# Turning the x tile of a token step: TensorE transposes, or VectorE's 32 x 32 blocks with sixteen DMA moves

## What is computed

```
hs = layernorm(x)                                # 4 sequences of 256 tokens
gate, xBC, dt = split(hs @ in_proj_w.T)          # 8192, 8192 + 2*8*128, 128 columns
xBC = silu(causal_conv(xBC, 4 taps) + conv_b)    # x: 128 heads of 64; B, C: 8 groups of 128
dt = softplus(dt + dt_bias);  A = -exp(A_log)
y[l] = sum over s <= l of (C[l] . B[s]) * exp(cumsum(dt A)[l] - cumsum(dt A)[s]) * dt[s] * x[s]  +  D * x[l]
out = rmsnorm(y * silu(gate)) * norm_w @ out_proj_w.T
```

## Time and profile before

| | |
|---|---|
| median of three runs | 1679.8 us (1677.4 to 1680.8) |
| the profiled execution | 1681.4 us, its span 1679.7 us |
| PE busy | 1643.6 us, 98% |
| DVE, ACT, POOL busy | 74%, 77%, 46% |
| DMA engines, mean | 98 to 99 GB/s over the span, queue of SP 30.9% |

### The profile page before, as it was taken

One profiled execution on the slowest core, in us unless ns is written; L12 is line 12 of the kernel. 1 busy time (PEld: TensorE's weight loads), 2 busy tenths in 40 slices (PEclk: granted clock), 3 DMA queues, 4 the chain that ended last, 5 costly groups with the idle time before them and its releaser, 6 DMA issues.

```text
span 1679.7 us, 27176 instructions
## 1 busy us (share of the span) xinstructions
PE 1643.6 (98%) x9464; PEld 1356.5 (81%) x9464; DVE 1244.7 (74%) x1975; ACT 1286.2 (77%) x2218; POOL 779.2 (46%) x806
## 2 busy tenths in 40 slices
PE   6999999999999999999999999999999999999998
PEld 4888777888888888888888888888888888888876
DVE  5887886777677767677767776776767777767886
ACT  4444559878888788869887788878887889689862
POOL 3565124454445355534544354444454545355470
PEclk9999999999999999999999999999999999999999
DMA  5320343233333323323323232323233333223421
GB/s 172 117 89 1 113 145 113 94 95 92 112 93 107 97 82 122 103 74 97 116 88 116 88 116 88 106 79 113 91 107 97 108 96 114 71 89 109 117 91 51
DMA packets 98662, 166.61 MB, mean 99 GB/s; under 512 B 11648, under 2 KB 49920, under 8 KB 96864
## 3 DMA queue, kind: packets, MB, share of 16 engines
q1 hardware_dynamic: 98528, 164.88, 30.9%
HBM read 158.56 MB, written 6.29 MB: 98 GB/s over the span
## 4 chain that ended last, share of the span: by engine, by line
PE 80%; DVE 5%; ACT 2%; issue 1%; POOL 1%; DVEq 0%; POOLq 0%; ACTq 0%
PE bank L156 15%; PE bank L158 15%; PE bank L157 14%; PE bank L2217 7%; PE bank L2251 7%; PE bank L2252 7%; PE bank L2255 7%; PE bank L2239 3%; PE bank L2203 3%; PE bank L2305 1%; ACT m_mt L1582 1%; DVE m_xc L1882 1%; DVE m_y L1961 1%; DVE m_y L1951 0%; DVE m_gate L1882 0%
## 5 line engine op out<-in xcount | busy, mean ns | idle before, releaser
L156 PE MATMUL bank<-xh,w_h 128*128 128x512 f32 x1152 | 469.1, 407 | 6.2 <-DVE m_xc L1882 3.7
L158 PE MATMUL bank<-xh,w_l 128*128 128x512 f32 x1152 | 452.6, 393 | 0.0
L157 PE MATMUL bank<-xl,w_h 128*128 128x512 f32 x1152 | 449.8, 390 | 0.0
L1489 POOL TENSOR_TENSOR m_z_l<-m_zg,m_z_h 128x512 fp32r<-128x512 f32 x128 | 188.1, 1469 | 472.9 <-ACT m_z_h L1636 472.9
L1582 ACT ACTIVATE m_mt<-m_mt,m_unit 128x128 f32<-128x128 f32 x1024 | 312.3, 390 | 0.0
L1471 POOL TENSOR_TENSOR w_l<-w_raw,w_h 128x512 fp32r<-128x512 f32 x142 | 184.8, 1302 | 265.2 <-ACT w_h L1549 265.2
L156 PEld LDWEIGHTS bank<-xh,w_h 128*128 128x128 f32 x1152 | 217.0, 188 | 57.5 <-issue 17.1
L158 PEld LDWEIGHTS bank<-xh,w_l 128*128 128x128 f32 x1152 | 216.6, 188 | 48.0
L1882 DVE SCALAR_TENSOR_TENSOR m_xc<-bank,m_par_conv,m_xc 128x1020 f32<-128x1020 f32 (+2 forms) x192 | 244.3, 1273 | 14.6 <-ACT m_xc L1561 10.1
L157 PEld LDWEIGHTS bank<-xl,w_h 128*128 128x128 f32 x1152 | 217.2, 189 | 39.7
L1893 DVE TENSOR_TENSOR x<-x,bank 128x512 f32<-128x512 f32 x128 | 87.7, 685 | 202.9 <-PE bank L2255 202.8
(11 more groups left out here) (315 smaller groups left out, 2871.4 us busy)
## 6 DMA issues: line engine op xcount, KB each, us to landing
m_mt<-ncs_rows SPq DMA_DIRECT2D x128, 512.0 KB, 4.5
w_raw<-w_in SPq DMA_DIRECT2D x144, 256.0 KB, 2.9
m_wo_raw<-w_out_in SPq DMA_DIRECT2D x64, 256.0 KB, 3.7
m_e<-ecs_rows SPq DMA_DIRECT2D x128, 128.0 KB, 3.5
a_wo_raw<-wo_in SPq DMA_DIRECT2D x8, 1024.0 KB, 4.9
x<-x_in SPq DMA_DIRECT2D x8, 256.0 KB, 5.1
a_wq_raw<-wq_in SPq DMA_DIRECT2D x8, 256.0 KB, 3.2
x_saved<-x SPq DMA_DIRECT2D x1, 2048.0 KB, 7.9
```

The lines of the kernel that those rows point to most:

```text
L156: nc.tensor.matmul(out, ah, bh, start=first, stop=False)
L157: nc.tensor.matmul(out, ah, bl, start=False, stop=False)
L158: return nc.tensor.matmul(out, al, bh, start=False, stop=last)
L1489: nc.gpsimd.tensor_tensor(z_l[:, s % 2, :, :], zg[:], f(z_h[:, s % 2, :, :]), ALU.subtract).then_inc(zl_ready, 1)
```

## The change

PE's turn and its two places in PE's step are removed. In its place turn_blocks on DVE transposes the 128 x 512 tile of xc in blocks of 32 x 32 into a new tile x_blocks (one buffer), with the channels reordered so that the four channel tiles are innermost. move_x on SP then issues sixteen DMAs of 32 partitions x 512 B that put each block row into its place in xdt (slots i % 2, i counted over the whole run), with four semaphores in turn. times_dt multiplies xdt in place by dt. As xdt and xdd now have the order (side, channel, tile), diag reads the weights of a head through of_head and across those of a tile through of_tile, both with a step of four elements. turned_in and scaled_in say in which step DVE does what: in odd step s it turns s+1 first of all and s+2 after make_z, in even step s it scales s in the place of the old times_dt, and s+1 after the taps. turn_blocks(i) waits until the moves of i-1 have landed. to_chunk_end of an even step runs in that step. across no longer waits for times_dt.

```
+            def move_x(g, s):
+                g, s = normal(g, s)
+                i = nth(g, s)
+                sp.wait_ge(x_turned, i + 1)
+                sp.wait_ge(diag_done, at(g, s - 2))
+                if s % 2 == 0:
+                    sp.wait_ge(xdd_ready, pair(g, s - 2))
+                if i < 2:
+                    sp.wait_ge(n.turned, NT)
+                for a in range(BLOCKS):
+                    for j in range(BLOCKS):
+                        sp.dma_start(xdt[j * BLOCK:(j + 1) * BLOCK, i % 2, a * P:(a + 1) * P],
+                                     x_blocks[a * BLOCK:(a + 1) * BLOCK, j, :, :].rearrange("r e c -> r (e c)")
+                                     ).then_inc(x_landed[i % X_SEMS], 16)
...
                         sp.wait_ge(wo_split, wo_at(g, half, k))
                         load_wo(g + half, 1 - half, k)
+                late_turn = kind == "last" and s >= NT
+                if s % 2 == 0 and (own(kind) and paired(kind, s) or kind == "last" and s == NT):
+                    move_x(g, s + 1)
+                if kind == "lead" and s == STEPS - 1:
+                    move_x(g, s + 1)
                 for done in masked_in(kind, s):
                     if ahead(kind, done + ROW_BUFS):
                         sp.wait_ge(diag_done, at(g, done))
                         load_rows(g, done + ROW_BUFS)
+                    if not late_turn and done % 2 == 0 and ahead(kind, done + 2):
+                        move_x(g, done + 2)
+                    if late_turn and done + 2 < STEPS:
+                        move_x(g, done + 2)
...
+            def turn_blocks(g, s):
+                g, s = normal(g, s)
+                half, t = divmod(s, NT)
+                i = nth(g, s)
+                if t == 0:
+                    dve.wait_ge(silu_done, conv_at(g - 1 + half, X_LAST[half]))
+                if i >= 1:
+                    dve.wait_ge(x_landed[(i - 1) % X_SEMS], X_COUNT * ((i - 1) // X_SEMS + 1))
+                nc.vector.transpose(x_blocks[:].rearrange("p j e c -> p j c e"), xc[:, half, :, t * P:(t + 1) * P].rearrange(
+                    "p c (j e) -> p j c e", e=BLOCK)).then_inc(x_turned, 1)
+
             def times_dt(g, s):
-                g, s = g + s // STEPS, s % STEPS
                 half, t = divmod(s, NT)
+                i = nth(g, s)
                 dve.wait_ge(unit_loaded[half], (g + 1) * 16)
-                dve.wait_ge(x_turned, at(g, s))
-                dve.wait_ge(diag_done, at(g, s - 2))
-                if s % 2 == 0:
-                    dve.wait_ge(xdd_ready, pair(g, s - 2))
-                nc.vector.tensor_tensor(xdt[:, s % 2, :].rearrange("p (h c) -> p h c", h=UH),
-                                        bank[:, 6, :].rearrange("p (h c) -> p h c", h=UH),
-                                        spread(unit[:, half, t * UH:(t + 1) * UH]), ALU.mult).then_inc(xdt_ready, 1)
+                dve.wait_ge(x_landed[i % X_SEMS], X_COUNT * (i // X_SEMS + 1))
+                x_sides = by_side(xdt[:, i % 2, :])
+                nc.vector.tensor_tensor(x_sides, x_sides, spread(unit[:, half, t * UH:(t + 1) * UH]),
+                                        ALU.mult).then_inc(xdt_ready, 1)
...
+                for made in turned_in(kind, s)[:1]:
+                    turn_blocks(g, made)
                 if behind(kind, s - 2):
                     add_out(g, s - 2)
...
                         make_y(g, made)
                         make_z(g, made)
-                if ahead(kind, s + 1) and s != STEPS - 1:
-                    times_dt(g, s + 1)
+                for made in turned_in(kind, s)[1:]:
+                    turn_blocks(g, made)
+                for made in scaled_in(kind, s)[:1]:
+                    times_dt(g, made)
...
                     scale_across(g, s, kind)
+                for made in scaled_in(kind, s)[1:]:
+                    times_dt(g, made)
...
-            def turn(g, s):
-                g, s = g + s // STEPS, s % STEPS
-                half, t = divmod(s, NT)
-                if t == 0:
-                    pe.wait_ge(silu_done, conv_at(g - 1 + half, X_LAST[half]))
-                pe.wait_ge(xdt_ready, at(g, s - 1))
-                pe.wait_ge(off_ready, pair(g, s - 2 if s % 2 == 1 else s - 4))
-                for ct in range(CT):
-                    last = nc.tensor.transpose(bank[:, 6, ct * P:(ct + 1) * P], xc[:, half, ct, t * P:(t + 1) * P],
-                                               ident[:])
-                last.then_inc(x_turned, 1)
-
...
-                                            xdt[:, s % 2, h * SP_:(h + 1) * SP_], mt[:, s % ROW_BUFS, h, :],
+                                            of_head(xdt[:, s % 2, :], h), mt[:, s % ROW_BUFS, h, :],
...
-                else:
-                    pe.wait_ge(xdt_ready, at(g, s + 1))
                 for ct in range(CT):
-                    last = nc.tensor.matmul(bank[:, across_bank(kind, s), ct * P:(ct + 1) * P], xdd[:, ct * P:(ct + 1) * P],
+                    last = nc.tensor.matmul(bank[:, across_bank(kind, s), ct * P:(ct + 1) * P], of_tile(xdd[:], ct),
                                             cb_across[:, s % NT // CHUNKS, :], start=True, stop=True)
```

```
+    def turned_in(kind, s):
+
+        if kind == "last" and s >= NT:
+            return [s + 2] if s + 2 < STEPS else []
+        return [s + 1, s + 2] if s % 2 == 1 and ahead(kind, s + 1) else []
+
+    def scaled_in(kind, s):
+
+        if kind == "last" and s >= NT - 1:
+            return [s + 1] if s + 1 < STEPS else []
+        return [s, s + 1] if s % 2 == 0 and own(kind) else []
```

More of the change, by code:

```diff
@@ L42 @@
 LEAD = 8
+BLOCK = 32
+BLOCKS = P // BLOCK
+X_SEMS, X_COUNT = 4, 16 * BLOCKS * BLOCKS
 W_BUFS, WO_BUFS, ROW_BUFS = 3, CT, 4
@@ L1028, in ssm_block @@
     wo_l = sb("wo_l", [P, CT, DIM], F32R)
+    x_blocks = sb("x_blocks", [P, BLOCKS, BLOCK, CT])
     ncs_units = ncs_dram.rearrange("t (g u h) s -> g u t h s", g=SG, u=2)
@@ L1144, in ssm_block @@
     x_turned = sem("x_turned")
+    x_landed = [sem(f"x_landed{i}") for i in range(X_SEMS)]
     xdt_ready = sem("xdt_ready")
@@ L1274, in across_bank, with nth @@
         return 0 if s == STEPS - 1 else 6
+    def nth(g, s):
+        return g * STEPS + s
     def normal(g, s):
@@ L1336, in _ @@
             sp.dma_start(dt_raw, w_dt.rearrange("p k h -> p (k h)")).then_inc(dt_loaded, 16)
-            for counted in (clamped, decay_ready, mt_ready, x_turned, xdt_ready, diag_done, y_ready, sq_ready,
+            for counted in (clamped, decay_ready, mt_ready, xdt_ready, diag_done, y_ready, sq_ready,
                             sq_summed, z_ready, zh_ready, zl_ready, out_done, acc_added):
@@ L1508, in step @@
                         w_low(g, m + 2)
-                if s % 2 == 1 and ahead(kind, s + 1):
-                    to_chunk_end(g, s + 1)
+                if s % 2 == 0 and own(kind):
+                    to_chunk_end(g, s)
                 if kind == "last" and s == NT:
@@ L2027, in step @@
                         make_z(g, made)
-                if kind == "lead" and s == STEPS - 1:
-                    times_dt(g, s + 1)
                 if ahead(kind, s + 2):
@@ L2036, in step @@
                     sums_to_scale(0)
-                if s == STEPS - 1 and kind in ("first", "middle"):
-                    times_dt(g, s + 1)
                 if kind == "lead":
@@ L2309, in step @@
             def step(g, s, kind):
-                if ahead(kind, s + 1) and s != STEPS - 1:
-                    turn(g, s + 1)
                 for ready in masked_in(kind, s):
@@ L2337, in step @@
                     project(g, m, 1)
-                if s == STEPS - 1 and kind != "last":
-                    pe.wait_ge(cb_across_ready, g + 2)
-                    turn(g, s + 1)
                 if behind(kind, s - 1):
```

12 lines of the change are left out of this document (8 added, 4 removed).

## The result

The changed kernel takes 2260.9 us (2255.3 to 2262.7, four runs) where the kernel before takes 1678.9 beside it: a ratio of 1.346, 95% interval 1.343 to 1.349. The forecast was 1918 us, 1810 to 2080. The sign was right, and so was the place of the loss; its size was wrong by a factor of 2.4: +238 us were forecast, +582 came.

The account below looks back on a forecast made before the run. TensorE bounded the kernel before; after, DVE waiting for moves would. Seven groups +186 us, last group +13 and +27, start +12: +238 on 1679.8 gives 1918 us, range 1810 to 2080, at 78%.

Parts of the forecast that it names:

- What leaves PE: 56 to 77 us: TensorE's four transposes per token step, removed over 128 steps: worth 56 to 77 us where TensorE sets the time.
- The move: M = 9.5 us: Sixteen DMAs on SP, from free to move until landed: 15 x 0.47 + 2.4 + 0.05 = 9.5 us, ends 7.8 and 12.3.
- the second rival: SP issues at the price of e, 0.62 us, so a move takes 12.3 us: about 2170 us; chance 12%.
- The turn: 0.60, ends 0.5 and 1.2: turn_blocks on DVE, the block transpose of one step: 0.60 us, with 0.5 and 1.2 as ends.
- The loop: Per pair of steps, DVE waits at the odd step's second turn: period 8.7 us plus move plus taps; 204.6 us a group.
- The second bound: Two moves in a row per pair, plus two turns, times_dt and mask: 19.0 + 3.1 = 22.1 us.
- Cost at nothing: Left out of the sum: waits taken off PE, to_chunk_end on GpSimd, mt loads ahead of move_x, strided weight loads.
- the bounds of +100 and +54: Weights 16 B apart on PE, if twice per column: +100 us for diag, +54 us for across; taken as nothing.
- The start and the last group: Outside the seven groups: start +12 us; last group's first three pairs +13, its second half +27 at 10.1 us a step.
- The second bound, SP: SP's queue: two moves a pair are 15 us, other issues about 3.5 us, fitting barely into 20 us.
- rival 1: DVE's 6 us of slack a pair cover the wait and PE stays the bound: about 1615 us; chance 5%.
- What would show it: Sixteen issues in 7 to 7.5 us, DVE idle 6 to 8 us, PE about 85% busy, clock near 1.00.

Follow-up runs that it names:

- the kernel with four moves and two tiles: The changed kernel in plain layout with four 128-row DMAs a step in place of sixteen, blocks not in transposed places, and two x_blocks: 1670.6 us, ratio 0.994.
- the probe: The kernel before with bursts of dead DMAs of differing rows, bytes and ends in SP's idle time: 0.63 us an issue inside SBUF, 0.44 from DRAM.
- the run with xdd first: The changed kernel with GpSimd's to_chunk_end of even steps placed ahead of the squares: 2253.3 us, ratio 1.341.
- with two block tiles: The changed kernel, still sixteen moves a step, with two x_blocks, so the turn of step i waits only for the moves of i-2: 2106.3 us, ratio 1.254.
- the dead moves: The kernel before with sixteen added SBUF moves a step on SP's queue into a tile nobody reads; only SP waits for them: 1909.8 us, ratio 1.137.

## Why the prediction was wrong

**What bounds the kernel.** Right. TensorE was the bound before, and the kernel with four moves and two tiles shows that it is again once the moves are hidden.

**What leaves PE: 56 to 77 us.** High, though the sum didn't use it. Sixteen turns a group are worth 5.9 us where nothing else stands in the way, 0.37 each; at that price 128 would be 47 us. The lower end, 0.44 from the chain, was the nearer one; the 77 us of the line overlap with other matmuls.

**The move: M = 9.5 us.** This is the step that failed. M was 11.3 = 15 x 0.63 + 1.8. The landing was quicker than the 2.4 taken, the issue dearer than the 0.47. The forecast went by the shape, 32 rows; the probe shows that rows and bytes don't matter, and that two ends in SBUF do. The argument for 0.62 stood in the text, as the second rival, "the address patterns on both sides are in SBUF", and was given 12%. The range had the same fault: its upper end was "M over some 11 us", and M was 11.3.

**The turn: 0.60, ends 0.5 and 1.2.** It took 1.10 (pitch 0.94 to 1.0), near the upper end; 0.71 when it writes contiguously. The Trainium skill ("VectorE: DVE Perf Modes", The three transpose paths) has 311 ns for 128 x 128 in bf16, from which the prediction's estimate of 1.24 us came; for float32 in one instruction, 0.71 is the number here, and 1.10 with the output 16 B apart.

**The loop.** The mechanism was right: the wait stands before turn(s+2) in odd steps, put to the DMA of xdt, and the period is DVE's work and M. For s = 5 the forecast's 25.8 becomes 30.35 by the timeline: M +1.8; two turns +0.75; y + e 1.25 in place of 0.73 and the mask 1.68 in place of 1.30, less 0.2 elsewhere, +0.7; and 1.3 in which the move waits for xdd (DVE goes on from the turn at 1339.4, xdd is done at 1340.62 and the move starts at 1340.70). In pairs of two moves (s = 3, 7, 15) M counts twice: 30.3, 27.0 and 27.1 measured where 22.1 were forecast. The group is 243.5; rival (2), which had M at 12.3 and the rest as forecast, came to 235.6. So about two thirds of the miss in a group (26 of 39 us: the sum with M = 11.3 and a turn of 1.0 is 230.8) come from the sizes of move and turn.

The rest lies mostly in s = 3 (30.3, and 26.5 by that sum), s = 5 (30.35 and 28.4) and s = 11 (33.2 and 29.1). In s = 3 and s = 5 the move waits for xdd. In s = 11 the forecast took the longer of two bounds, one move with all of DVE's work, or two moves without the taps; the timeline of DVE has two moves and one tile of taps in a row:

```profile
1426.01 1.48 DVE L1970 TENSOR_TENSOR xdt<-xdt,m_unit 128x512 f32<-128x512 f32 x1 [3.15 <-DMA xdt<-m_x_blocks]
1427.41 2.33 DVE L1991 TENSOR_TENSOR m_mt<-m_mt,m_cb 128x1024 f32<-128x1024 f32 x1
1429.66 3.89 DVE L1939 SCALAR_TENSOR_TENSOR m_xc<-bank,m_par_conv,m_xc 128x1020 f32<-128x1020 f32 x3
1433.46 1.11 DVE L1961 STREAM_TRANSPOSE m_x_blocks<-m_xc 128x512 f32<-128x512 f32 x1
```

DVE stands until the second move has landed, and the scaling, the mask, the taps (3.80) and the turn all come behind it. The second bound with these taps is 26.5 + 3.8 = 30.3.

**Cost at nothing.** "If GpSimd were late, across would be by an instruction of it, about 1 us" had the wrong thing late: it is the move of the even step, since it waits for xdd too, and then everything behind it. SP waits for xdd 39.3 us in the run, 25.0 of them in the last group's second half (the line below). In the steady groups the wait couldn't be had back by order, as the run with xdd first shows. In the pair s = 5 DVE's instructions beside GpSimd's are slow as well. times_dt, which read PSUM, now has both inputs in SBUF, and once it took 1.81 us in place of 0.68, beside this one of GpSimd:

```profile
1304.60 1.30 POOL L1546 TENSOR_TENSOR m_z_l<-m_zg,m_z_h 128x512 fp32r<-128x512 f32 x1 [4.46 <-ACT m_z_h L1693]
```

The Trainium skill ("SBUF — State Buffer", SBUF: two separate sides) has a DVE instruction with two SBUF inputs and a GpSimd instruction that reads SBUF take turns at a port pair for whole instructions; the trace agrees in that times_dt, started at 1304.64, ends 0.55 us after GpSimd's. But this is rare: two of the 128 times_dt take over 1 us, and all together they hold DVE 90.1 us against 87.3 before, the masks 165.7 against 170.3. As a cause of the loss it is small. The strided loads, taken as hidden, were hidden here, and cost 75 us where TensorE is the bound; the bounds of +100 and +54 held them.

**The start and the last group.** The start was about right (+9 for +12). The second half of the last group was forecast with 10.1 us a step; it took 17.1 (120.0 / 7). There the sum left out that the move of an even step waits for xdd. SP's waits in that half (2080:2200):

```profile
SPq L1410 <- POOL m_xdd L1539: 25.0, 3, 9.4
```

GpSimd makes xdd behind its work on z, z comes from DVE, and DVE stood at the turn until the odd step's move had landed. So the two moves of a pair run one after the other with this chain between them: even moves start at 2109.65 and 2143.39, the odd one between at 2122.24. With M = 4.7 this half takes 71.7 us (two block tiles) or 77.2 (one), so that even then it costs 24 us and more, about as much as its waits for xdd (24.2). That kernels with a short M pay it was not in the prediction.

**The second bound, SP.** "SP itself still fits into 20 us, barely" failed with the issue price: with two block tiles two moves take 21.2 us of the queue (10.24 + 10.91), and 5.4 are left for all else, forecast at 3.5, in a period of 26.5. Hidden moves (rival 1) were judged by DVE's slack alone; the dead moves show +230 us with no wait of DVE for a move. On both bounds sixteen issues are too many.

**What would show it.** Idle time of 6 to 8 us before turn(s+2) was 9.6; PE at 85% was 80%; the sixteen issues of 7 to 7.5 us took 10.1 to 10.8, which is the sign that the text named for a wrong size. The clock did not stay near 1.00: it was 0.92 in the group, in which TensorE stood 48 of 243.5 us, and 0.90 over the run.

## What to carry to other kernels

Count the issues of a transfer and price each by a row with the same two ends, SBUF to SBUF or DRAM to SBUF, before one with the same number of rows or bytes; where no such row exists, let the range reach to the dearest issue shown. A transfer that replaces work of the bounding engine must fit twice, into the issuing queue's period and into the loop between the buffer's release and its next use. Where two waits stand in a row in one period, the work behind each adds to both. Removing one wait shows the next. And sum the start and the last, unpipelined stretch on their own: what hides in the steady loop stands bare there.

## What the runs showed of the hardware

- A DMA between two places in SBUF costs 0.60 us of SP's queue, 0.63 with its gap, for 16 B, 512 B or 4 x 128 B a row, for 32 and for 128 rows; with its source in DRAM 0.42 to 0.44 in the same bursts, but 0.61 for the halves of e; from SBUF to DRAM, alone in the queue, 0.38. Landing in SBUF from SBUF takes 1.8 us for 16 KB, 2.6 for 64 KB.
- 256 KB written to DRAM in runs of 128 B land in 5.5 us (median), up to 10.4.
- A block transpose of 128 x 512 float32 on DVE takes 0.71 us, and 1.10 if the output's neighbours are 16 B apart.
- A load of 64 weights 16 B apart takes 209 ns in place of 137, one of 128 takes 329 in place of 191; the products then take 66 and 218 ns each on the chain in place of 59 and 112 (2.12 / 32, 1.74 / 8, 1.90 / 32, 0.56 / 5).
- Two DVE instructions of the same form can differ nearly threefold beside GpSimd: times_dt with both inputs in SBUF took 0.66 to 1.81 us; with one input in PSUM it took 0.67 to 0.69.
